# One engine only gathers, one-hot masks by a different instruction, and a reordered attention block in a two-layer GNN kernel

## The reference

```python
# layer 1: mean over incoming edges, then a dense product
neigh_sum = segment_sum(x[src], dst)
mean = neigh_sum / maximum(deg, 1)
neigh_agg = where(deg > 0, mean, x)
x = layernorm(x + relu(concat([x, neigh_agg]) @ W.T + b))
# layer 2: attention over incoming edges, 4 node types, 8 edge types
Q, K, V = (type_matmul(x, W_, node_type) for W_ in (W_Q, W_K, W_V))
k_t = type_matmul(K[src], W_edge, edge_type)
scores = sum(Q[dst] * k_t, -1) / sqrt(128) * mu[edge_type]
attn = sparse_softmax(scores, dst)
x = layernorm(x + segment_sum(V[src] * attn[:, None], dst))
```

## Time and the profile before

| | us |
|---|---|
| median of 3 runs | 3593.15 |
| lowest and highest | 3582.03, 3596.72 |
| the profiled execution's own time | 3594.51 |
| span in its trace | 3592.7 |

### The profile page before, as it was taken

How to read it: one execution, slowest core, us unless ns; L and a number is a source line. 1 busy time by engine, 2 the same in 40 slices (tenths; PEclk the granted TensorE clock), 3 DMA queues, 4 the chain that set the end, 5 groups by cost and what they waited for, 6 DMA issues and landing times.

```text
span 3592.7 us, 38408 instructions
## 1 busy us (share of the span) xinstructions
PE 2618.7 (73%) x13802; PEld 1868.6 (52%) x13802; DVE 1554.8 (43%) x4730; ACT 1151.8 (32%) x2057; POOL 2244.9 (62%) x2302
## 2 busy tenths in 40 slices
PE   3587888887878827777777777777777777777777
PEld 1355566555556625555554555555555555555555
DVE  8476677666667613322322233322322333323223
ACT  4344454444444412222222222222222222222222
POOL 7665566566556454666666666666666666666664
PEclk9799999899999968777778887777777877777778
DMA  6244354444444432333333333333333333333332
GB/s 157 62 129 121 111 144 130 120 126 120 119 119 126 118 122 75 100 99 100 100 100 101 103 100 100 99 97 100 100 100 102 102 100 101 100 99 100 101 100 69
DMA packets 256960, 384.03 MB, mean 107 GB/s; under 512 B 100640, under 2 KB 189003, under 8 KB 250625
## 3 DMA queue, kind: packets, MB, share of 16 engines
q0 software_dynamic: 108112, 273.13, 27.6%
q1 hardware_dynamic: 146833, 107.53, 9.7%
q10 hardware_dynamic: 1824, 0.92, 0.1%
HBM read 304.30 MB, written 77.13 MB: 106 GB/s over the span
## 4 chain that ended last, share of the span: by engine, by line
POOL 36%; PE 25%; issue 18%; another core or an unknown queue 13%; DVE 5%; ACT 2%; DMA 0%; ACTq 0%; DVEq 0%; POOLq 0%
POOL ring L722 35%; PE banks L777 9%; PE banks L769 4%; PE banks L803 3%; PE banks L850 1%; PE banks L862 1%; PE banks L992 1%; PE banks L855 1%; PE banks L1005 1%; ACT picks L1138 1%; PE banks L1029 1%; PE banks L865 1%; PE banks L1021 1%; POOL ring L717 1%
## 5 line engine op out<-in xcount | busy, mean ns | idle before, releaser
L722 POOL DMA_INDIRECT ring<-kv_table,src_n x1563 | 1485.4, 950 | 798.3 <-issue 447.6
L1005 PE MATMUL banks<-identf,ring 128*128 128x128 f32 x1568 | 436.9, 373 | 630.4 <-issue 501.1
L717 POOL DMA_INDIRECT ring<-x_part_rows,work x462 | 475.1, 1028 | 307.4 <-PE banks L803 142.8
L1005 PEld LDWEIGHTS banks<-identf,ring 128*128 128x128 f32 x1568 | 250.9, 182 | 791.1 <-issue 585.2
L777 PE MATMUL banks<-sums,picks 128*126 128x385 bf16 x2401 | 608.1, 342 | 33.3 <-ACT picks L1138 15.3
L1138 ACT ACTIVATE picks<-banks 128x343 bf16<-128x343 f32 x882 | 433.3, 512 | 543.7 <-PE banks L769 333.6
L1227 ACT ACTIVATE work<-banks 128x512 f32<-128x512 f32 x392 | 213.5, 598 | 887.6 <-remote 638.9
L1623 DVE SCALAR_TENSOR_TENSOR sums<-sums,corr,banks 128x128 f32<-128x128 f32 x98 | 34.0, 347 | 1029.2 <-remote 1022.6
L1219 ACT ACTIVATE work<-banks,negmax 128x2048 f32<-128x2048 f32 x98 | 192.8, 1968 | 807.9 <-issue 743.7
L777 PEld LDWEIGHTS banks<-sums,picks 128*126 128x126 bf16 x2401 | 331.6, 143 | 149.4 <-issue 54.1
L769 PE MATMUL banks<-sums 128*128 128x343 bf16 x882 | 286.1, 325 | 168.7 <-issue 105.8
(11 more groups left out here) (260 smaller groups left out, 2363.3 us busy)
## 6 DMA issues: line engine op xcount, KB each, us to landing
kv_table<-ring SPq DMA_DIRECT2D x48, 1024.0 KB
ring<-kv_table,src_n POOLq DMA_INDIRECT x1563
sums<-x_typed SPq DMA_DIRECT2D x99, 128.0 KB
x_typed<-work SPq DMA_DIRECT2D x49, 256.0 KB
ring<-x_part_rows,work POOLq DMA_INDIRECT x462
x_part_rows<-sums SPq DMA_DIRECT2D x7, 675.5 KB, 7.1
src_n<-x_part_rows,work POOLq DMA_INDIRECT x224
sums<-x_rows SPq DMA_DIRECT2D x51, 64.0 KB
```

Source lines behind the costliest of these rows:

```text
L717: pool.indirect_dma_start(near[k % RUNS][:, j, :], None, part_dram, bass.IndirectOffsetOnAxis(ap=col_ids[:, first + j:first + j + 1], axis ...
L722: pool.indirect_dma_start(kv_ring[u][:, j, :], None, table, bass.IndirectOffsetOnAxis(ap=of, axis=0)).then_inc(l1_rows[2 * u + j // RUN], 16)
L1005: tr = pe.transpose(bank[KEY_BANK[g]][:, j * P:(j + 1) * P], kv_ring[k.u][:, g * 4 + j, 0:D], identf[:, :])
```

## The change

1. `belong` makes its matrix by seven `tensor_scalar` instructions of 128x128 with one bf16 tensor as input (`iota_g` becomes bf16) in place of one `tensor_tensor` of 128x896 with two f32 inputs.
2. POOL's two pieces of arithmetic go to DVE: `weights` in step 0 (8 instructions), `edge_keys` in steps 1 and 2 as four `scalar_tensor_tensor` of 416 columns. The third run buffer lies in `spare_n` instead of `src_n`. The digits come in 27 parts of 512 or 640 columns in steps 4 to 30, later within a step, and are stored before tile 30.
3. In layer 1 the times in `PICK_AT` are other ones, the first one-hot wait of the next step moves from the last h to h = 2 of the step after, ACT's small copies move by one to three picks, and `normalise_x1` moves from the end of a step to the start of the next.
4. In layer 2 PE's order is other, `transpose_keys` is cut into halves, and the waits and banks (`KEY_BANK`, `PROB_BANK`) follow:

The core of the diff:

```diff
-        iota_g = sb("iota_g", [P, P])
+        iota_g = sb("iota_g", [P, P], BF16)
-        near_runs = [..., src_n[:, 0:HALF * TW // 2].bitcast(F32)]
+        near_runs = [..., spare_n[:, 0:HALF * TW // 2].bitcast(F32)]
-        KEY_BANK = (4, 5, 6, 4)
-        PROB_BANK = (5, 6, 4, 5)
+        KEY_BANK = (4, 5, 4, 5)
+        PROB_BANK = (6, 4, 5, 6)
...
             for k in range(2 * ND):
-                if k == RUNS - 1:
-                    edge_keys()
-                    pool.wait_ge(keys_nat, 1)
-                if k == RUNS:
-                    weights()
...
-            PICK_AT = [-(-c * TILES // GCOLS) for c in range(GCOLS)]
+            PICK_AT = [3, 4, 7, 10, 14, 17, 18, 19, 22, 24, 25, 28, 29, 31, 33, 37, 42, 44]
...
-                    if i + 2 < ND and h == TILES - 1:
-                        wait_hot(i + 2, 0)
+                    if 0 < i < ND - 1 and h == 2:
+                        wait_hot(i + 1, 0)
...
-                    if k.b == 0 and g > 0:
-                        pe.wait_ge(keysT_ready, g + 1)
+                    elif g >= 2:
+                        pe.wait_ge(keysT_ready, k.b * 4 + g + 1)
...
+                        if half == 1 and k.b > 0:
+                            pe.wait_ge(prob_copied, k.b * 4 - 1)
+                        pe.wait_ge(l1_rows[2 * k.u + half], (k.fill * RUN + rows_of) * 16)
...
-                    if g == 0 and not ahead:
+                    if g == 0:
                         pe.wait_ge(prob_ready, k.b + 1)
                     elif g < 3 and ahead:
-                        pe.wait_ge(keysT_ready, (k.b + 1) * 4 + (g + 2))
+                        pe.wait_ge(keysT_ready, (k.b + 1) * 4 + g)
...
-                dve.tensor_tensor(belongs[h], col_keys[...].broadcast_to([P, HALF, P]),
-                                  iota_g[...].broadcast_to([P, HALF, P]), ALU.is_equal)
+                for j in range(HALF):
+                    ins = dve.tensor_scalar(belongs[h][:, j, :], iota_g[:, :], col_keys[:, 1, first + j:first + j + 1], None,
+                                            ALU.is_equal)
...
+            def weights():
+                for e in range(ET):
+                    dve.tensor_scalar(we_s[:, e, :], we_s[:, e, :], mu_b[:, e:e + 1], SCALE, ALU.mult, ALU.mult)
+            def edge_keys(k):
+                dve.scalar_tensor_tensor(key_f[:, at], src_n[:, at], float(ET), et_n[:, at], ALU.mult, ALU.add)
```

## The result

The changed kernel takes 3684.73 us (median of 4 runs, 3681.31 to 3700.17) against 3589.63 (4 runs, 3582.03 to 3596.72): ratio 1.0283, interval 1.0242 to 1.0324. It is slower by 95 us, where I forecast 3560; 3684.73 lies above my range too.

A forecast was written before the change was run, and what follows sets the result against it. Layer 1 bound by PE and POOL, about half each; layer 2 by POOL's gathers plus a late release. 3594.5 - 11 - 22 + 0 = 3561.5, given as 3560 us; own range 3530 to 3583, 8-in-10 range 3440 to 3680.

The forecast's parts named there:

- The start: Steps 0 and 1: taking `weights` and `edge_keys` off POOL's path gains 11 us, between 3.6 and 13.6.
- Layer 2: Layer 2's blocks: only order changes, 5 us of cover hide a `score` 0.2 us later; 0 taken, gain bound -288.
- rival A: Layer 2: the values are seen in time and POOL restarts at once; 3272 us, in part around 3420; chance 0.15.
- Layer 1: Layer 1's steps: -27 us for shorter gathers beside the new `belong`, +5 for picks, together -22.
- The step that failed: Layer 1, `belong`: POOL's gathers get shorter at unchanged DVE time, paying in half the runs: 27 us, bounds 0 and 55.
- Rival C: Layer 1: denser picks press on two banks, ACT's unmatched waits of 138.0 us per 1000 double; 3716 us; chance 0.08.
- My own price for the picks: Layer 1: adjacent picks come each 0.6 us against ACT's 0.51 copy, thin slack; 0.1 us a step, 5 us.
- Rival E: Layer 1: by the shared-ports rule the new one-hots hold POOL's runs 1.1 us each; +24, 3606 us; chance 0.03.

## Why the prediction was wrong

The forecast was one sum, 3594.5 - 11 - 22 + 0.

**The start: right.** -10.8 by the windows against the -11 taken.

**Layer 2: right in its sum.** 2209.4 and 2209.2 us. POOL's wait stayed at 3.2 us and rival A fell. What I did not price is that each gather takes 9 to 11 ns more; on a late chip POOL's wait absorbs it, in time it shows: 1563 x 11 ns = 17 us, more than the whole difference of 15 us there.

**Layer 1: -22 in the sum, +100.8 us by the windows.** The step that failed is "`belong`... DVE's time is unchanged... It can pay only where POOL isn't waiting for PE, about half the runs: 27 us". Its observation was right: from 200 to 1200 us the 122 gathers that overlap an L1414 take 1281 ns on average and the other 468 take 968, and without it the gathers average 975 ns. Its price was wrong in sign. The runs show the mask alone at +159 us on a late chip and +18 to 20 on chips in time, and the change without it at or under the kernel before. I took half of the gathers' saving as time because POOL waited for PE in half of the runs. But on a chip in time POOL, with 0.30 us ahead of each gather, and PE are both full, so a shorter gather ends in a wait for PE, and DVE's cost was 1.15 us against 1.01, not "the same". I had set the distance between starts of the new instructions against the duration of the old one, 1.09. On the late chip the step grows with the waits for PE's results, which I had seen in the earlier trace rows and treated as layer 2's alone.

**Rival C** had the symptom (the third adjacent pick waiting for its bank) and priced it at +156; I gave it 0.08. Its sign came, 197.9 us of ACT's unmatched waits per 1000 against 138.0, and the gaps stand there, 103.9 us of them, but the picks' times are not their cause by themselves: with the old mask most are gone. My own price for the picks had a misreading in it. I put adjacent picks 0.6 us apart, from an average over a step that counts the dense products too; in the changed kernel's trace two of them start at 605.63 and 605.94, 0.31 apart.

**Rival E**, the shared ports of the Trainium skill's "SBUF — State Buffer", section "Who interferes with whom", would have held the gathers; they became shorter in layer 1, from 1028 to 975 ns. The trace does not agree with it for these instructions: the 144 gathers beside the new mask take 981 ns on average, the other 402 take 974. I had given that section only in part. The Trainium skill says there too that a DVE instruction with two SBUF inputs contends with a GpSimd instruction that reads SBUF. The slow gathers beside L1414, 1281 ns, fit that if an indirect gather counts as such a reader, which no run here tests.

What remains open is the mechanism below the mask. In every late trace PE pauses with nothing named and its results are seen late, and in none from a chip in time. That the new mask puts this in step with POOL's runs of gathers is read from two traces and not tested, and as 2 us more on ACT moved the kernel before by 58 us, any edit that shifts the phases might do the like; why some chips are late was not settled.

## What to carry to other kernels

An engine that finishes sooner is worth nothing until the engine it waits for has room: price the relief by how full the next engine is, and price the instructions that pay for it by their distance from start to start, the old one's like the new one's. Where readers see an engine's results microseconds after its last instruction, treat this as a limit of every stage, and test a small edit alone, since it moves all phases against each other. And run an experiment beside its own baseline on the same chip: one part of this change cost 0.6% on one chip and 4.5% on another.

## What the runs showed of the hardware that I had not expected

- The same program took 3012 to 3014 us on two chips and 3581 to 3651 on two others, with equal durations of instructions in the two traces of before (a `values` series of 32 passes 3.79 us on either). On the first two PE never pauses over 0.5 us without a named wait in the stretches I counted, and its results are read at once. In the comparison's late trace of before it has 338 such pauses in layer 2, and its results are read up to 7.5 us late in layer 1 and 9 us in layer 2, there about 3 us after POOL's last gather.
- On chips in time each indirect gather of layer 2 took 946 ns with POOL's arithmetic in its program and 956 to 957 with that moved away, all through layer 2, long after that arithmetic. Putting back the weights alone didn't restore it.
- On a late chip, 2 us of additional waiting on ACT in each step made the kernel 58 us faster.
- An indirect gather beside one DVE comparison with two inputs (128x896, f32 in) took 1281 ns on average against 968 for the others; beside seven with one bf16 input of 128x128 it took 981 against 974.
